# Masks of two row maxima added by TensorE in PSUM, plain maxima on VectorE, 64-row score products, and the router's logits moved behind the second dense layer

## The reference, cut to what matters

```python
# layer 0, on xn = layernorm(x); 16 heads of 8 features
lin = causal linear attention with a Taylor feature map
win = softmax(q k / sqrt(8)) over keys t-64 .. t, times v
x = x + xn + concat(lin, win) @ Wout + dense4(xn)     # 128 -> 512 -> 512 -> 512 -> 128, ternary weights
# layer 1, on xn = layernorm(x)
scores = q k / sqrt(8), causal                        # 16 heads of 8 features
x = x + softmax(scores) @ v @ Wo + bo + mixture(xn)   # 8 experts, the 2 largest of logits = xn @ Wg.T
```

## Time and profile before

| | us |
|---|---|
| median of 3 runs | 1279.28 |
| lowest and highest | 1278.79 to 1283.72 |
| the profiled execution | 1290.89 |
| its span, first to last instruction | 1289.1 |
| share of the higher TensorE clock, mean | 0.965 |

### The profile page before, as it was taken

The page is one execution under the profiler, slowest core; times in us unless marked ns, Lnnn a source line. Parts: engine busy times, 40 slices in busy tenths (PEclk is TensorE's granted clock), DMA queues, the critical chain, the costliest instruction groups (busy, mean ns, idle before and its releaser), DMA issues.

```text
span 1289.1 us, 26679 instructions
## 1 busy us (share of the span) xinstructions
PE 1165.4 (90%) x9122; PEld 750.8 (58%) x9122; DVE 865.2 (67%) x3433; ACT 743.5 (58%) x1580; POOL 649.6 (50%) x846
## 2 busy tenths in 40 slices
PE   5989999999999899989998999899989867988997
PEld 2445754565457545754575457545764456884896
DVE  4066588658865885688658865786578755885563
ACT  2356367735773577457745774477546624557675
POOL 4475254535444454545454544454445436675577
PEclk9998999999999899999999999899989969999999
DMA  7601620162015301540154015401472016542233
GB/s 237 153 3 54 177 73 12 54 184 73 13 55 147 108 15 39 151 120 15 39 152 117 17 39 151 117 17 39 139 211 64 5 26 142 82 70 29 41 55 40
DMA packets 123961, 105.53 MB, mean 82 GB/s; under 512 B 15242, under 2 KB 118578, under 8 KB 123826
## 3 DMA queue, kind: packets, MB, share of 16 engines
q1 hardware_dynamic: 102162, 85.89, 24.7%
q0 software_dynamic: 13792, 9.54, 5.1%
q10 hardware_dynamic: 7872, 8.39, 1.9%
HBM read 58.59 MB, written 46.37 MB: 81 GB/s over the span
## 4 chain that ended last, share of the span: by engine, by line
PE 49%; DVE 21%; ACT 13%; issue 8%; POOL 6%; DMA 2%; DVEq 0%; SPq 0%; POOLq 0%; ACTq 0%
PE bank L700 14%; PE heads L765 11%; ACT probs L1117 8%; PE bank L679 6%; PE bank L707 6%; DVE xnT_s L1585 4%; DVE hrow L1585 4%; DVE hT_s L1585 3%; POOL out L1362 3%; PE bank L690 2%; PE bank L675 2%; DVE spare L1585 2%; PE bank L1050 2%; PE bank L684 1%; PE bank L815 1%
## 5 line engine op out<-in xcount | busy, mean ns | idle before, releaser
L1117 ACT ACTIVATE probs<-bank 128x512 f32<-128x512 f32 (+2 forms) x896 | 441.2, 582 | 176.6 <-PE bank L707 169.8
L1309 POOL TENSOR_SCALAR_AFFINE_SELECT probs<-probs 128x384 f32<-128x384 f32 x256 | 127.7, 521 | 242.1 <-ACT probs L1117 242.1
L765 PE MATMUL heads<-probs,V 128*18 128x192 f32 (+9 forms) x3072 | 194.6, 394 | 10.7 <-POOL probs L1312 4.6
L707 PE MATMUL bank<-K,Q 128*128 128x192 bf16 (+4 forms) x1024 | 199.2, 271 | 4.3 <-ACT probs L1117 0.2
L707 PE MATMUL bank<-Q,K 128*128 128x192 bf16 (+4 forms) x1024 | 175.0, 275 | 16.3 <-ACT probs L1117 7.0
L1362 POOL DMA_INDIRECT out<-h1T_s x78 | 123.2, 1580 | 60.3 <-ACT h1T_s L1270 37.4
L765 PEld LDWEIGHTS heads<-probs,V 128*9 128x9 f32 (+1 forms) x3072 | 78.2, 94 | 122.3 <-issue 85.4
L1262 ACT ACTIVATE h2T_s<-bank,h1T_s 128x128 f32<-128x128 f32 x312 | 89.2, 368 | 93.1 <-PE bank L1050 80.9
L707 PEld LDWEIGHTS bank<-Q,K 128*128 128x128 bf16 x1024 | 81.4, 99 | 87.5 <-ACT probs L1117 31.1
L707 PE MATMUL bank<-QM,K 128*128 128x512 bf16 (+3 forms) x512 | 121.5, 301 | 7.8 <-DVE gatesT_s L1545 1.4
L707 PEld LDWEIGHTS bank<-K,Q 128*128 128x128 bf16 x1024 | 85.2, 98 | 67.7 <-DVE mx_c L1585 14.3
(11 more groups left out here) (241 smaller groups left out, 2285.1 us busy)
## 6 DMA issues: line engine op xcount, KB each, us to landing
K<-slots_of_k SPq DMA_DIRECT2D x64, 256.0 KB, 4.2
Q<-slots_of_q SPq DMA_DIRECT2D x15, 1024.0 KB, 10.9
QM<-slots_of_qm SPq DMA_DIRECT2D x8, 1024.0 KB, 9.4
h1T_s<-sorted_rows SPq DMA_DIRECT2D x78, 65.0 KB
slots_of_q<-Q SPq DMA_DIRECT2D x8, 384.0 KB, 2.6
slots_of_k<-QM SPq DMA_DIRECT2D x8, 384.0 KB, 2.9
slots_of_qm<-Q SPq DMA_DIRECT2D x8, 384.0 KB, 2.6
slots_of_k<-Q SPq DMA_DIRECT2D x8, 384.0 KB
```

The lines of the kernel that those rows point to most:

```text
L707: mm = pe.matmul(to[:, at:at + right.shape[1]], left, right, start=True, stop=True, skip_group_check=True)
L765: mm = pe.matmul(heads[ROWS * i:ROWS * i + n, P * j:P * j + widths[j]], V[:, j, g // 2, i, first:first + n], slot_of(kind, 2 * g + i // 2) ...
L1117: return act.activation(to, bank, func, scale=scale, bias=bias).then_inc(taken_sem(run, unit), 1)
L1309: pool.affine_select(out=three, in_=three, compare_op=ALU.is_ge, fill=0.0, base=0, pattern=[[0, 3], [1, P]], channel_multiplier=-1)
```

## The change

Four edits:

1. **Masks on TensorE.** A third operand, a bf16 identity, turns the mask into a product: `add_mask` multiplies identity and mask into the bank, in the same accumulation as the scores. A `cmax` unit gets one such instruction behind its scores (128 columns for one diagonal block, 256 for the units with two blocks). An `smax` unit gets one of 384 columns ahead of its scores.
2. **Plain maxima.** `row_max` is a `tensor_reduce` with maximum, without a mask and without the scratch output. An `smax` unit and a 256+256 `cmax` unit need one instruction in place of two.
3. **64 rows.** All score products of a single head take only its own 64 partitions (`own(h)`), so they use the upper or the lower half of the array's rows. The units that hold both heads (every fifth) stay at 128 rows. The units are put in another order: heads alternate from unit to unit, even first in `lin` and `causal`, odd first in `cmax`.
4. **Logits.** `logits` is issued behind `h2_3`.

On TensorE also: in the first batch it waits for the masks before `third_layer`.

```diff
+HEADS_OF = {"lin": (0, 1), "causal": (0, 1), "cmax": (1, 0)}
 def tri_units(tag):
-    return [f"{tag}{u}" for p in range(H // 2) for u in (f"{2 * p}a", f"{2 * p}b", f"{2 * p + 1}a", f"{2 * p + 1}b", f"_{p}")]
+    return [f"{tag}{u}" for p in range(H // 2) for u in [f"{2 * p + i}{half}" for half in "ab" for i in HEADS_OF[tag]] + [f"_{p}"]]
...
-    units += ["hT2", "k2", "q2", "xnT2", "v2", "logits"] if this else []
+    units += ["hT2", "k2", "q2", "xnT2", "v2"] if this else []
     units += ["h2_3"] if after else []
+    units += ["logits"] if this else []
...
+            def add_mask(to, mask, first):
+                return pe.matmul(to, ident_b[:, :], mask, start=first, stop=not first, skip_group_check=True)
+            def own(h):
+                return slice(SROWS * (h % SH), SROWS * (h % SH + 1))
...
             def slide_max(run, n):
+                add_mask(to[:, 0:2 * WQ].rearrange("p (j c) -> p j c", c=WQ), mask, True)
+                for j in tiles:
+                    first, at = (0, WIN) if j == 0 else (P * j - WIN, WQ * (j % 2))
+                    right = K1[own(h), h, first:P * (j + 1)]
+                    mm = pe.matmul(to[:, at:at + right.shape[1]], q_part(Q1, h, P * j, P), right, start=False, stop=True, skip_group_check=True)
...
             def causal_max(run, n):
+                for at, left, right in parts:
+                    pe.matmul(to[:, at:at + right.shape[1]], left, right, start=True, stop=False, skip_group_check=True)
+                mask = causal_neg[:, :].unsqueeze(1).to_broadcast([P, diagonal.shape[1], P])
+                add_mask(diagonal, mask, False).then_inc(full_sem(run, CMAX_UNITS[n]), 1)
...
                 project_rows(run, "v2", hT, wv1[:, :])
+                if after:
+                    dense_low(run, "h2_3", layer2, 3)
                 wait_taken(run, "xnT2")
                 project_rows(run, "logits", xnT, wgT[:, :], E)
-                if after:
-                    dense_low(run, "h2_3", layer2, 3)
...
-            def row_max(run, unit, parts):
+            def row_max(run, unit, to, columns):
                 dve.wait_ge(full_sem(run, unit), full_at(run, unit))
-                for to, at, mask in parts:
-                    last = dve.tensor_tensor_reduce(beside[:, at:at + n], bank_of(run, unit)[:, at:at + n], mask, 1.0, NEG, ALU.add, ALU.max, to)
+                last = dve.tensor_reduce(to, columns, AX_X, ALU.max)
                 last.then_inc(taken_sem(run, unit), 1)
```

More of the change, by code:

```diff
@@ new lines, in own, with q_part, slide_unit @@
+            def own(h):
+                return slice(SROWS * (h % SH), SROWS * (h % SH + 1))
+            def q_part(buf, h, a, n, of=None):
+                return buf[own(h) if of is None else of, h // SH, a:a + n]
+            def slide_unit(n):
+                half = n % 4 // 2
+                return 2 * (n // 4) + n % 2, (2 * half, 2 * half + 1)
+            def slide_max(run, n):
+                h, tiles = slide_unit(n)
+                to = to_bank(run, SMAX_UNITS[n])
+                mask = slide_neg[:, :, :] if 0 in tiles else slide_neg[:, 1:2, :].to_broadcast([P, 2, WQ])
+                add_mask(to[:, 0:2 * WQ].rearrange("p (j c) -> p j c", c=WQ), mask, True)
[3 more added lines that the diff above has]
+                    mm = pe.matmul(to[:, at:at + right.shape[1]], q_part(Q1, h, P * j, P), right, start=False, stop=True, skip_group_check=True)
+                mm.then_inc(full_sem(run, SMAX_UNITS[n]), 1)
@@ L740, in tri_scores @@
                 scores_into(run, units[n], parts)
             def slide_scores(run, n):
-                h, parts = n // 2, []
-                for j in (2 * (n % 2), 2 * (n % 2) + 1):
-                    parts.append((WQ * (j % 2), K1[:, h, P * j:P * (j + 1)], q_part(Q1, h, P * j, SLIDE_N[j])))
+                (h, tiles), parts = slide_unit(n), []
+                for j in tiles:
+                    parts.append((WQ * (j % 2), K1[own(h), h, P * j:P * (j + 1)], q_part(Q1, h, P * j, SLIDE_N[j])))
@@ L995, in dense_stage @@
                 project_rows(run, "v2", hT, wv1[:, :])
+                if after:
+                    dense_low(run, "h2_3", layer2, 3)
                 wait_taken(run, "xnT2")
                 project_rows(run, "logits", xnT, wgT[:, :], E)
[L998 to L1000 removed]
+                if not after:
                     run_tiles(QUERIED, ROUTED)
```

89 lines of the change are left out of this document (44 added, 45 removed).

## The result

The changed kernel takes 1363.5 us (1358.5 to 1370.4, 4 runs) beside 1279.0 for the kernel before. The ratio is 1.0645, 95% interval 1.0615 to 1.0676, so it is 84 us slower. The forecast was 54 us slower, with a range up to 1352. The direction and the largest term were right. The size was not: it was 30 us short.

A forecast was written before the change was run, and what follows sets the result against it. VectorE bounds the `cmax` part by a little, TensorE close behind. Seven full pairs stages +45, first batch +5, tail +4, slide stage 0: 1279.3 + 54 = 1333 us, range 1254 to 1352 (the forecast case's own 1305 to 1350).

The forecast's parts named there:

- Price of a change: Each change between half rows and whole costs TensorE 0.10 us, 12.7 us from first `cmax` to slide stage.
- Signs (1) and (2): Starts come about 0.1 us after a mask's end, likewise before it; two 512-column half products start a few ns apart.
- (3): In the changed profile, the plain maximum of a 384-column unit starts 0.48 us after the one before.
- Sign (5): `cmax` part and last third together take about 64 us, with VectorE now waiting for a bank TensorE fills.
- sign (4): `v2`'s last product to pairs stage takes about 3.8 us at full clock; first `cmax` follows about 12 us later, not 8.8.
- First `cmax` to slide stage: TensorE needs 61.3 us, becomes the bound; with waits the stretch takes 64.6 instead of 55.6 us, +9.0 a batch.
- The logits and the opening: Logits behind `h2_3` let the first `cmax` start 2.5 us earlier a batch, limited by q2's fetch and GpSimd's row copies.
- Slide stage: Heads alternate without masks: -1.2 us of products against 16 changes, +1.6, taken as 0.
- First batch and tail: First batch +5 us for masks and 64 changes; tail +4 us, a third of its masks and 88 changes showing.
- changes cost nothing: Rival: at +0 a change TensorE needs 48.6 us in the stretch, VectorE stays the bound; 1251 us, chance 0.20.
- changes cost half: Rival: 0.05 us a change, 6.3 us less in the stretch; about 1283 us, chance 0.13.
- Halves don't overlap: Rival: products of the two row halves don't run at once, 27 us more; 1360 us, chance 0.07.

The follow-up runs named there:

- `more_changes`: Changed kernel with every mask that covered two tiles split in two, so product and mask take turns: 1471.4 us, ratio 1.147.
- `whole_rows`: Changed kernel with all score products over all 128 rows again, masks on TensorE, new order and logits kept: 1279.8 us, ratio 0.9876.
- `masks_twice`: Changed kernel with each mask product issued twice in a row: 1417.5 us, ratio 1.092.
- `logits_only`: Kernel before with only the logits moved behind `h2_3`: 1280.0 us, ratio 0.988; repeated on two other chips, ratios 0.9965 and 0.9964.
- `after_third`: Changed kernel with the third layer ahead of the 5th unit of maxima: 1352.4 us, ratio 1.054.
- `logits_back`: Changed kernel with the logits in front of `h2_3` again: 1385.2 us, ratio 1.078.
- `own_rows`: Kernel before with 64-row score products in the new order of units, masks still on VectorE, logits where they were: 1298.5 us, ratio 1.0006.
- `third_whole`: Changed kernel with all score products over 128 rows and the third layer ahead of the 5th unit of maxima: 1275.5 us, ratio 0.9948.

## Why the prediction was right or wrong, point by point

1. **Price of a change (0.10 us each way): right.** It is +0.10 in the timeline on both sides of a mask and 0.11 by `more_changes`, and in `whole_rows`, without any change, the stretch's growth is gone. By the rule of the Trainium skill, "TensorEngine Tiling (Array Packing)", section "Key Properties", the change of mode drains TensorE; the trace agrees and gives it a size. `weigh`'s rows were the right ones to read it from; the 32-row transpose was not, because it counts with the whole array: behind it the next product starts 0.11 us later in `whole_rows`, where that product takes all rows, and 0.205 us later in the changed kernel, where it takes half of them.
2. **Masks, 0.42 ns a column: right,** 0.416 by `masks_twice`. **Halves overlap: right.** Signs (1) and (2) came as forecast, and so did (3): the second reduction of a `cmax` unit starts 0.46 to 0.48 us after its 384-column one. Sign (5), 64 us with VectorE waiting for TensorE, came too (63.9). Of sign (4) the first half came (3.7 us), the second (12 us) not quite: 12.8 to 14.2.
3. **First `cmax` to slide stage, +9.0: measured +7.3 to +7.7.** The prediction's 55.6 us ended with TensorE's first slide product, the 56.6 here with ScalarE's first slide instruction, about 1.0 later; so its 64.6 stands against about 62.9. If TensorE's need of 61.3 us stands, the waits on top were 1.6 us, not 3.3; the trace bears that out, since TensorE's weight loads stood 1.5 us for other engines there. The term was too high by 9 to 12 us in seven batches, against the sign of the miss. The prediction's own range was also added up wrongly at its upper end: with 0.12 a change and 5 us of waits its stretch is 68.8 us, 13.2 more, less 2.5, times 7, and 9 for the rest, which gives 1363 and not 1350. That this is the measured time is luck: a change cost 0.10, the waits were 1.6, and the time went elsewhere.
4. **The logits and the opening, -2.5: wrong, measured -0.5 and +0.4.** This is the step that failed. The words were: "The masks of the opening's 12 `smax` units ... fit into the rest", and the changes that these masks bring were put at nothing: the prediction counted changes of the opening in the first batch alone. The masks, 1.9 us, did fit: in `whole_rows`, with the masks and without changes, the way to the first `cmax` is 15.5 us, shorter than in `logits_only`. The changes did not. The trace has 25 between half rows and whole in each opening, 2.4 us by point 1, and with them the way is 17.3 and 17.7, 1.8 to 2.2 more (1.0 more in batches at full clock; in the others the low clock falls into the opening). `after_third` and `logits_back` show the opening at 11.5 and 11.4 us without a pause, where it was 8.8.

   Taken in the order of the sum: masks and changes without the logits edit (`logits_back`, 19.6 us) cost 1.8 to 2.3 us a batch over the kernel before, for which the sum had 0, and the logits edit then gives 1.9 to 2.3, for which it had 2.5. Together the step missed by 2.0 to 2.9 us a batch, 14 to 20 us.

   In the kernel before, the same edit is worth only 0.36%, 4.6 us and not 17.5. There the logits behind `h2_3` lay VectorE's ranking bare, ahead of the maxima in its order, so that the gap moved from in front of the pairs stage into it. What is late next was thus VectorE's ranking, neither q2 nor GpSimd's copies.
5. **Slide stage, 0: wrong, +1.4 to +2.0.** At full clock it is 29.8 against 29.1, +0.8, and that comes with the half rows: `own_rows` has 29.9 at full clock and `whole_rows` 29.1. The rest is the clock: TensorE was at 0.57 of full from 549.5 to 557.5, at the end of the slide stage, in every second batch. Of the low clock I had written that the wait for `xnT2` goes and so no fall comes. It doesn't come there; it comes elsewhere, and the mean of the execution is 0.964 against 0.965 before. 10 to 14 us in all.
6. **The base.** I added the difference to the median. The profiled execution of before lay 11.9 us above its median, that of after 1.4 below. This is 13 of the missed 30 us. (In two later traces of before it lay 4.0 and 2.5 us above.) Part of it is that first trace's own: four of its seven batches took 18.4 to 18.6 us to the first `cmax`, three in each later trace, and it was from such a batch that I read the gain of the logits. The executions at the median were not profiled, so that they hold less of it is argued, not shown. What makes the kernel before take 1279 us on one chip and 1297 on another I can't say.
7. **First batch and tail: right** within 3 us.

For the first pair of traces the steps add up: 54 forecast, +14 for point 4, +10 for point 5, +13 for point 6, -12 for point 3, +2 for point 7, together 81 of the 84 us.

The rivals "changes cost nothing" and "changes cost half" fell with point 1. "Halves don't overlap" gave 1360, close to what was measured, and was still wrong: the time was right for another reason.

## What to carry to other kernels

Before splitting the array's rows, count how often the new order goes from part to whole and back, stage by stage, and price each at what the nearest existing change in the trace costs; here 127 of them ate 12 us a batch where the overlap gave 4 by the prediction's count. A mask product between products of another shape pays it twice. When work is moved to fill a wait, look at what the awaited engine does next: the wait may reappear one step later, and the cheapest cure was then to put independent work (the third layer) into it. And compare the profiled execution with the medians: where it is slower, as by 11.9 us here, a gain read from one of its batches can be too large.

## What the runs showed of the hardware that was not expected

- Products of the two row halves start mostly 3 to 7 ns apart in the changed kernel, although a product of 512 columns alone takes 215 ns.
- At a change between half rows and whole the next weight load isn't hidden: it starts 0.30 us after the product before it (600.35 to 600.65), where in `whole_rows` it starts at once (559.44).
- TensorE's granted clock fell to 0.53 in a stretch in which the profile shows it busy 11.00 of 11.00 us, in `more_changes`, where what it did before was small products with a change at almost every one. The 0.1 us of a change lies inside the recorded duration of the product before it (0.38 us from 600.35, with the next start at 600.66), so the profile shows it as busy. That the changes are why the clock fell isn't shown.
- The low clock moved with the edits. In the kernel before it lies at the end of the dense stage, in the changed one in the opening's third layer and at the end of the slide stage; the mean stayed at 0.96. `third_whole` (0.982) and `whole_rows` (0.977) had the least of it, `more_changes` (0.946) the most.
- A product whose mask lies in another mode shows no idle time: both waits of 0.1 us are inside the starts, and the idle column of the 320 causal masks stays at 0.0.
